# A two-layer convolution with group norms: the head's weight work reordered, its sums shortened, TensorE's constant waits without increments

## What is computed

```
# group norm: 32 groups of 2 channels, over the whole image
y  = x + G @ (pw @ (A @ depthwise3x3(gn(x))))     # A = softmax(attention), G = softmax(global)
out = y + conv3x3(sign(gn(y)), sign(clip(w)) * mean|clip(w)|)
```

## Time and profile before

| | |
|---|---|
| median of 3 runs | 1862.25 us (1861.27 to 1868.79) |
| profiled execution, its own time | 1867.16 us |
| its span | 1865.3 us |
| TensorE busy | 1767.8 us (95%) |
| VectorE, ScalarE, POOL busy | 1603.3 (86%), 1333.6 (71%), 580.4 us (31%) |
| HBM read and written | 134.95 and 134.22 MB |

### The profile page before, as it was taken

The page is one execution under the profiler, slowest core; times in us unless marked ns, Lnnn a source line. Parts: engine busy times, 40 slices in busy tenths (PEclk is TensorE's granted clock), DMA queues, the critical chain, the costliest instruction groups (busy, mean ns, idle before and its releaser), DMA issues.

```text
span 1865.3 us, 76406 instructions
## 1 busy us (share of the span) xinstructions
PE 1767.8 (95%) x33132; PEld 1535.2 (82%) x33132; DVE 1603.3 (86%) x2605; ACT 1333.6 (71%) x1460; POOL 580.4 (31%) x353
## 2 busy tenths in 40 slices
PE   0299999999999999999999999999999999999997
PEld 0299987799888887889988888779988888889996
DVE  5878889888998889888898888988899888877776
ACT  2277777677777776777777777777777777677774
POOL 1133333233233332333333333323333333333331
PEclk9999999999999999999999999999999999999999
DMA  9725665556555665656655666556655655433234
GB/s 283 194 81 159 158 152 143 153 153 154 148 150 163 154 153 143 158 149 155 158 138 160 159 156 154 142 159 153 153 146 155 164 151 153 103 82 75 74 77 103
DMA packets 278624, 271.39 MB, mean 145 GB/s; under 512 B 16112, under 2 KB 278320, under 8 KB 278464
## 3 DMA queue, kind: packets, MB, share of 16 engines
q1 hardware_dynamic: 269568, 260.11, 54.1%
q10 hardware_dynamic: 8448, 8.39, 1.6%
q0 software_dynamic: 448, 0.73, 0.2%
HBM read 134.95 MB, written 134.22 MB: 144 GB/s over the span
## 4 chain that ended last, share of the span: by engine, by line
PE 85%; DVE 8%; DMA 3%; issue 2%; ACT 2%; ACTq 0%; SPq 0%; DVEq 0%
PE psA L511 73%; PE psB L511 12%; DMA ring<-in_x 3%; DVE bnt L734 2%; DVE ring L944 1%; ACT xh L388 1%; DVE ring L910 1%; DVE psL L940 1%; DVE pk L921 1%; DVE aggr L848 1%; DVE xc L902 1%; ACT xn L384 0%; ACT xc L357 0%; DVE sums L750 0%; DVE ring L949 0%
## 5 line engine op out<-in xcount | busy, mean ns | idle before, releaser
L511 PE MATMUL psA<-xh,W 64*64 64x512 f16 x17912 | 1552.4, 373 | 15.6 <-DVE xh L969 6.6
L511 PEld LDWEIGHTS psA<-xh,W 64*64 64x64 f16 x17912 | 1080.9, 106 | 137.6 <-issue 71.3
L511 PE MATMUL psA<-xl,W 64*64 64x512 f16 x9216 | 989.9, 376 | 0.7 <-issue 0.6
L307 POOL TENSOR_TENSOR xl<-xc,xn 128x1024 f16<-128x1024 f32 (+1 forms) x320 | 570.8, 1794 | 1203.5 <-ACT xn L384 1187.9
L511 PEld LDWEIGHTS psA<-xl,W 64*64 64x64 f16 x9216 | 593.5, 107 | 38.1 <-issue 2.3
L511 PE MATMUL psB<-pk,W 64*64 64x512 f16 (+1 forms) x4944 | 604.9, 362 | 2.3 <-DVE pk L921 1.9
L388 ACT ACTIVATE xh<-xc 64x1024 f16<-64x1024 f32 (+2 forms) x622 | 574.5, 941 | 9.2
L384 ACT ACTIVATE xn<-xc 128x1024 f16<-128x1024 f32 (+2 forms) x262 | 270.8, 1036 | 278.1 <-PE psA L511 199.5
L910 DVE SCALAR_TENSOR_TENSOR ring<-psA,columns,ring 128x1024 f32<-128x1024 f32 x256 | 328.4, 1283 | 142.1 <-PE psA L511 141.9
L511 PEld LDWEIGHTS psB<-pk,W 64*64 64x64 f16 x4944 | 301.0, 106 | 64.8 <-issue 51.3
L734 DVE BATCH_NORM_STATS2 bnt<-ring 128x6 f32<-128x512 f32 x512 | 325.7, 681 | 30.7 <-DMA ring<-in_x 30.1
(11 more groups left out here) (104 smaller groups left out, 109.6 us busy)
## 6 DMA issues: line engine op xcount, KB each, us to landing
out_y<-ring SPq DMA_DIRECT2D x512, 256.0 KB, 3.3
ring<-in_x SPq DMA_DIRECT2D x448, 256.0 KB, 4.0
ring<-in_x SPq DMA_DIRECT2D x16, 512.0 KB, 16.8
ring<-in_x ACTq DMA_DIRECT2D x16, 512.0 KB, 16.5
pk<-in_w1T POOLq DMA_DIRECT2D x2, 144.0 KB, 7.2
ring<-in_w1n POOLq DMA_DIRECT2D x2, 144.0 KB, 8.0
grp<-in_same_group POOLq DMA_DIRECT2D x1, 64.0 KB, 7.3
ring<-in_dw POOLq DMA_DIRECT2D x2, 2.2 KB, 6.7
```

Source lines behind the costliest of these rows:

```text
L307: ins = nc.gpsimd.tensor_tensor(xl[:, slot:slot + rows, 1:W + 1], xc[:, j:j + rows], xn[:, k:k + rows, 1:W + 1], ALU.subtract)
L511: mm = pe.matmul(bank[out0:out0 + C, c0:c1], weights[src0:src0 + C, :], src[src0:src0 + C, slot:slot + rows, width[0]:width[0] + width[1]] ...
```

## The change

- Attention weights are loaded under a semaphore of their own (attention_in), and VectorE waits for them behind piece 0 instead of for all twelve loads behind piece 3. The softmax, GT/U2 and MT steps move up by one to two pieces.
- w1T and w1n (four loads) get a semaphore too and are issued by POOL once piece 1 has landed. VectorE waits for them ahead of the mean of |w|, ScalarE ahead of the signs.
- ScalarE issues halves 6 to 9 (before: 6 to 8) behind the exponentials, and 10 and 11 behind the W1 copies.
- SP waits for piece 13 ahead of the first load of the second image's chunks.
- TensorE waits for the remaining weight loads itself.
- The sums of the statistics are shortened (factors 0.25, 4 and XSCALE are folded into others); two side results are taken behind the ones that TensorE waits for. This is so for every image.
- TensorE's increments of bank_turns remain only where the count is a register, that is in loops.

```diff
@@ sync
+            sp.wait_ge(piece_in[NPIECES - 3], 32)
             for g in range(NC, RING):
                 load_chunk(g)
@@ gpsimd
-            for dst, src in weights:
+            for k, src in enumerate((att, gatt)):
+                nc.gpsimd.dma_start(attx[:, k, :], src).then_inc(att_in, 16)
+            for dst, src in ((pwt, pwT), (idt, ident), (grp[:], same_group), (member[:], members), (dwt[0:C], dw),
+                             (dwt[C:128], dw)):
                 nc.gpsimd.dma_start(dst, src).then_inc(w_in, 16)
...
+            pool.wait_ge(piece_in[1], 32)
+            for dst, src in ((w1t[0:C], w1T), (w1t[C:128], w1T), (w1m[0:C, :], w1n), (w1m[C:128, :], w1n)):
+                nc.gpsimd.dma_start(dst, src).then_inc(w1_in, 16)
             pool.wait_ge(amax_rdy, 1)
@@ scalar
-            load_pieces(6, 9)
-            act.wait_ge(w_in, 16 * 12)
+            load_pieces(6, 10)
+            act.wait_ge(w1_in, 16 * 4)
...
-            load_pieces(9, 12)
+            load_pieces(10, 12)
@@ tensor
+            pe.wait_ge(w_in, 16 * 6)
             pe.wait_ge(gt_rdy, 1)
...
+            def turn(count):
+                if not isinstance(count, int):
+                    pe.sem_inc(bank_turns, 1)
             def bank_free(sem, count):
                 pe.wait_ge(sem, count)
-                pe.sem_inc(bank_turns, 1)
+                turn(count)
@@ vector, stats_parts
-                nc.vector.tensor_copy(sums[:, img % 2, 0:1], aggr[:, 0:1])
-                nc.vector.reduce_sum(sums[:, img % 2, 2:4], colp[:] if img > 0 else edge_columns(0, H // 2), AX.X)
                 nc.vector.tensor_scalar(aggr4[:, 0, :], member[:], aggr[:, 0:1], None, ALU.mult)
                 nc.vector.tensor_scalar(aggr4[:, 1, :], member[:], aggr[:, 1:2], None,
                                         ALU.mult).then_inc(aggr_rdy, 1)
+                nc.vector.tensor_copy(sums[:, img % 2, 0:1], aggr[:, 0:1])
+                nc.vector.reduce_sum(sums[:, img % 2, 2:4], colp[:] if img > 0 else edge_columns(0, H // 2), AX.X)
```

More of the change, by code:

```diff
@@ L169, in conv_preact @@
         nmean1 = (nmean_even, nmean_odd)
+        att_in = sem("attention_in")
         w_in = sem("w_in")
+        w1_in = sem("w1_in")
         piece_in = [sem(f"piece_in{p}") for p in range(NPIECES)]
@@ L761, in stats_piece @@
                 return ins
-            for p in range(4):
-                stats_piece(p)
-            dve.wait_ge(w_in, 16 * 12)
+            stats_piece(0)
+            dve.wait_ge(att_in, 16 * 2)
             for k in range(2):
@@ L769, in _ @@
                 link(nc.vector.tensor_scalar(small[:, k, 1:2], small[:, k, 0:1], -1.0, None, ALU.mult))
-            stats_piece(4)
+            stats_piece(1)
+            stats_piece(2)
             dve.wait_ge(exps, 2)
@@ L775, in _ @@
             ins.then_inc(gt_rdy, 1)
-            stats_piece(5)
+            stats_piece(3)
+            stats_piece(4)
             dve.wait_ge(prep_mm, 1)
@@ L780, in _ @@
             nc.vector.tensor_copy(U2[:, 1, :], psB[0:C, 0, 0:C]).then_inc(u_rdy, 1)
-            stats_piece(6)
+            stats_piece(5)
             dve.wait_ge(prep_mm, 2)
             nc.vector.tensor_copy(MT, psB[:, 1, 0:C]).then_inc(mt_rdy, 1)
+            stats_piece(6)
+            dve.wait_ge(w1_in, 16 * 4)
             link(nc.vector.tensor_scalar(w1m, w1m, 1.0, -1.0, ALU.min, ALU.max))
@@ L832, in link @@
                     dve.wait_ge(self.sem, self.count)
-            STATS_STEPS = 15
+            STATS_STEPS = 10
             def take_part(g):
@@ L857, in stats_of_group @@
                 steps = Steps(stats_chain, STATS_STEPS, img, 1)
[L858 to L864, removed]
+                nc.vector.reduce_sum(st[:, 3:4], psL[:, 0, 4:8], AX.X)
+                steps.link(nc.vector.reduce_sum(st[:, 2:3], psL[:, 0, 0:4], AX.X))
+                steps.link(nc.vector.tensor_scalar(st4[:, 0, :], psL[:, 0, 0:4], 4.0, st[:, 2:3], ALU.mult,
+                                                   ALU.subtract))
+                steps.link(nc.vector.scalar_tensor_tensor(out=st4[:, 1, :], in0=st4[:, 0, :], scalar=0.25,
+                                                          in1=st4[:, 0, :], op0=ALU.mult, op1=ALU.mult,
+                                                          accum_out=st[:, 4:5]))
+                nc.vector.tensor_scalar(st[:, 5:6], st[:, 4:5], st[:, 3:4], EPS, ALU.add,
+                                        ALU.add).then_inc(var_rdy, 1)
             def scale_of_group(img):
-                steps = Steps(stats_chain, STATS_STEPS, img, 7)
+                steps = Steps(stats_chain, STATS_STEPS, img, 4)
                 dve.wait_ge(xc_rdy, img * NC)
@@ L872, in scale_of_group @@
                 steps.link(nc.vector.reciprocal(st[:, 7:8], st[:, 6:7]))
[L873 to L877, removed]
+                steps.link(nc.vector.scalar_tensor_tensor(out=st[:, 9:10], in0=st[:, 5:6], scalar=st[:, 7:8],
+                                                          in1=st[:, 7:8], op0=ALU.mult, op1=ALU.mult))
+                steps.link(nc.vector.tensor_scalar(st[:, 10:11], st[:, 9:10], -0.5 * XSCALE, 1.5 * XSCALE, ALU.mult,
+                                                   ALU.add))
+                steps.link(nc.vector.tensor_tensor(rstd0[:], st[:, 10:11], st[:, 7:8], ALU.mult))
             def border_of_group(img):
-                steps = Steps(stats_chain, STATS_STEPS, img, 14)
+                steps = Steps(stats_chain, STATS_STEPS, img, 9)
                 steps.link(nc.vector.scalar_tensor_tensor(out=parts6[:, 0, :], in0=counts[:], scalar=mean0[:, 0:1],
```

15 lines of the change are left out of this document (6 added, 9 removed).

## The result

| | before | changed |
|---|---|---|
| median of 4 runs | 1863.51 us (1861.27 to 1868.79) | 1844.72 us (1843.51 to 1845.76) |
| profiled execution, its own time | 1867.16 us | 1843.51 us |
| its span | 1865.3 us | 1841.7 us |

A forecast was written before the change was run, and what follows sets the result against it. TensorE's products were taken to bound the kernel, with time to gain in the head and TensorE's gaps. Head 10.2, boundaries 4.0 and block borders 3 sum to 17.2 us, off the median 1862.25: 1845.0 us, range 1839 to 1853.

The forecast's parts named there:

- 1 and 3, last piece: Head: ScalarE's load queue stays filled and VectorE follows, so the last piece's statistics end 8.9 us earlier.
- 2, SyncE's wait: Head: waiting for piece 13 keeps chunk loads from competing with the last halves; priced at nothing by itself.
- 4, chain: Head, behind the last piece: two operations leave the path, sums and scale get shorter; 1.3 us saved.
- 5, boundaries: Seven image boundaries: the shorter chain reaches ScalarE 0.7 us sooner, TensorE's six gaps go; 4.0 us saved.
- 6, carried waits: TensorE's steps outside loops: directly worth 0, but shifted block borders leave two long images; 3 us saved.
- rival A: Head load: the rate is the same whoever fills it, only chunk bytes leave; head gains 5.0, 1850 us; chance 0.12.
- Rival D: TensorE: carried waits do nothing and the boundary gap stays, ScalarE late otherwise; 10.2 us alone, 1852 us; chance 0.06.
- rival C: TensorE starved of instructions: every border of each loop's first pass costs 1.3 us; slower, 1880 us; chance 0.02.

The follow-up runs named there:

- x7: The kernel before with only the head's new order (loads, maxima, ScalarE's halves, SyncE's wait), old sums and all increments: 1860.62 us, ratio 0.9965.
- x10: The changed kernel without SyncE's wait for piece 13 ahead of the second image's chunk loads: 1844.59 us.
- x8: The kernel before with only the shortened sums of the statistics: 1861.36 us, ratio 0.9974.
- x2: The kernel before with only TensorE's constant waits changed (increments kept where the count is a register): 1857.06 us.
- x1: The changed kernel with TensorE's increments put back outside the loops (342 instructions more): 1854.67 us.
- x11: The changed kernel with VectorE's maxima behind piece 3 again and softmax, copies and MT one to two pieces later: 1849.1 us.
- x12: The changed kernel with SyncE's wait moved from piece 13 to the last piece: 1844.05 us.
- x3: The kernel before with 124 increments ahead of TensorE's first wait, in idle time, which move only the block borders: 1867.3 us, ratio 1.000.
- x4: The changed kernel with 70 increments ahead of TensorE's first wait, borders at 147, 139 and 131 instructions into loops of images 1, 4 and 7: 1843.93 us.
- x5: The changed kernel with every constant wait outside the loops an instruction of its own again, but without an increment: 1853.93 us.
- x9: The changed kernel with, outside loops, the three waits on TensorE's own semaphores standing alone; the two xl waits carried behind an increment: 1853.36 us.
- x6: The changed kernel with an increment ahead of every constant wait outside the loops, single waits still carried by the products: 1843.74 us.

## Why the prediction was right, and where it was not

| step | forecast | measured |
|---|---|---|
| 1 and 3, last piece | 8.9 | 7.9 (profile), 7.7 (x7) |
| 2, SyncE's wait | 0 by itself | 0.3 at most (x10) |
| 4, chain | 1.3 | 1.4 (profile), 1.3 (x8) |
| 5, boundaries | 4.0 | 0.6 to 0.7 us an image (below), 3.9 in six |
| 6, carried waits | 3 | 9.7 (x2), 10 (x1) |
| sum | 17.2 | 23 (profile 23.7) |

**Steps 1 to 3.** The mechanism holds. x11 takes away the early maxima alone and finds's 207 again, so idle time of a queue is lost time, and rival A falls with it. By the Trainium skill, DMA: Bandwidth & Descriptors, Rules for kernel authors, a full second queue of disjoint halves should have brought nothing; x11 and the earlier trace rows disagree, 207 against 347 GB/s. The size was 1 us too large, in "the other 14.3 MB at 347 take 41.2 us, to 56.2, and landing adds 1 to 2". The bytes came out nearly as said: from 15 to 25 us the rate was 317, not 347, while the w1 loads ran (0.9 us lost), but in the first 15 us, without them, it was 232 and not 216 (0.24 MB or 0.7 us gained), so that they do change places. What was too small is the end, taken as 1.8 us (58.0): the rate fades and the last piece was usable at 58.5 to 59.2, 2.1 us or more behind 56.4 (x12 and the six profiles named at x10). That nothing should compete with the last halves was worth 0.3 us at most: "its worth is in the 8.8" named a cause that was not one. Two readings were off without an effect on the sum: ScalarE's queue was not empty yet when the half at 25.06 was issued, and 216 GB/s is the rate of the first 15 us in the earlier trace rows, with both queues at work, not of a lone queue.

**Step 4** was right to 0.1 us.

**Step 5** was right. In x2, which has neither the new sums nor issue gaps, images 1 and 2 take 220.02 and 219.91 us:

```profile
301.69:521.71 220.02, 219.54 (x4145) 191.26 (x4142) 196.67 (x326) 165.28 (x178) 70.98 (x40) 1.00 0.59 153
521.71:741.62 219.91, 219.34 (x4145) 195.27 (x4142) 196.47 (x326) 165.43 (x178) 70.98 (x40) 1.00 0.60 154
```

and 219.39 and 219.35 in the changed kernel. Images 3 to 5 take 219.81 in x2 and 219.14 in the changed kernel: 0.6 to 0.7 a boundary. Rival D falls. (x8, with the sums alone, gained 5.0 us, 3.7 beyond the 1.3 of its head.)

**Step 6 failed**, in two sentences. That "directly this is worth 0" looked only at the products, which are indeed back to back over such waits; it did not ask what the wait does to the fetching ahead. And "Now they fall first at 47, 214, 128, 40, ...: only images 2 and 5 resemble the bad ones" made the border's place the whole cause. x3 shows the place to be a cause and x4 shows that it is one only together with bare waits: borders at 131 to 147 without a gap. The term was 10 us where 3 was taken, outside its own bound of 8. Its opposite, rival C, had put all four borders of all eight loops at 1.3 us; nothing of that was seen. The prediction's places are also counted wrong by a constant. Laid against TensorE's records in order, the product behind each gap of image 1 stands 93, 348, 605 and 861 instructions into the loop, not 137, 394, 649 and 905 (the one at 353.30 us has five pairs of xl products between itself and the first xn product, which fixes it in the step). All places in the prediction and the expectations are some 44 too high, and the distances between them, on which the argument rests, stay. Of the crossing of a 16 KiB boundary the Trainium skill, Runtime: NRT & Kernel Launch, Instruction fetch mechanics, says that its cost is mostly hidden. With carried waits the runs agree (103 blocks, no gap); with TensorE's own waits bare, 7 to 11 gaps show (before, x1, x3, x5, x7 to x9), 10 us in all.

**Why the total came out.** By luck in part. 7 us too little in step 6, 1 too much in step 1, which would give 1839; the rest is the value subtracted from. The median of 1862.25 stood 4 to 5 us below what later groups gave (1866.4 to 1867.4; the parts timed alone, 5.8 in x7, 5.0 in x8 and 9.7 in x2, add up to 20.5 of the 22.0 between 1866.72 and 1844.72), and its runs lie 7.5 us apart, those of the changed kernel 2.3; that the issue gaps are what varies is likely, since x2 and x4, which have none, lie 2.3 and 1.1 apart, but it was not measured by itself. The number was right; of its reasons the first five were, but for what SyncE's wait is worth.

**What stays open.** What in a bare wait on TensorE's own semaphore makes it ask late for the next block. One reading fits, that TensorE stops there until products just issued are done, while a_added and suma_ready may have been reached long before; it was not tested. Nor was the queue against the half of the partitions (x11). Inside the loops the waits still stand alone, and there packets are up to 4.1 us late in the changed kernel too, without a gap (the unrolled steps: 2.0 at most). The lateness grows over a bare stretch, in image 1 of x1 from 1.7 us to 5.2; so in a longer loop body it might cost something, which was not tried.

## What to carry to other kernels

Where an engine works back to back and its program is long, look at whether "issue" gaps sit in a loop's first pass, and try carrying its waits before moving code about, first those on its own semaphores: TensorE stalled here on instructions it had yet to fetch. Then look in the built program at which waits the products really carry: one with two semaphores to wait for kept one of them bare. In a load-bound head, find what the queue that runs dry is waiting for; one small operation three pieces too late cost 4.4 us here. And time one part alone before believing in a sum: a term 7 us too small was hidden by a starting value 4 to 5 us too low and a term 1 us too large.

## What the runs showed of the hardware that was not expected

- The packet of a 16 KB block starts when TensorE passes the border of the block before it (median 0.2 us behind it in the changed kernel). With the waits on its own semaphores standing alone, it started up to 5.5 us behind that (x1, image 1: 1.7 us for the first unrolled block, 5.2 for the last of the loop's first pass).
- An instruction that only increments a semaphore costs TensorE nothing that shows: 6 a step in 68 steps, 1843.74 us (x6).
- A waiting instruction without an increment costs as much as one with it: 1853.93 (x5) and 1854.67 us (x1). It matters which wait it is: three on TensorE's own products a step, 1853.36 us (x9); two on VectorE's semaphores a step, 1844.72 us and no gap (the changed kernel).
- A load from two full queues does not end at its full rate: 344 GB/s at 55 us, 94 at 56.5, 25 at 57.5, last packet 58.0, usable 58.5 (x12).
- A queue that is filled late stays silent for longer than the delay: a half issued at 25.06 us, 1.1 us before the queue's last packet, started at 31.87 (before; issued at 24.84, started at 31.56 in x11). The other queue alone moved 207 GB/s meanwhile, with all 16 DMA engines busy.
- 0.59 MB of weights, issued by POOL beside two full queues, brought the rate from 346 GB/s (before, 15 to 25 us) to 317 (changed, the same stretch).
